# Attention's context kept with features on partitions up to the output projection; softmax denominators inverted by way of DMA hops and applied on GpSimd

## The reference, cut to what matters

```
x = x + layernorm(attention(layernorm(x)))
x = x + layernorm(experts(layernorm(x)))
```

```
scores = einsum('bhqd,bhkd->bhqk', q, k) / 4        # masked with -inf
ctx    = einsum('bhqk,bhkd->bhqd', softmax(scores), v)
out    = ctx.reshape(B, S, D) @ w_o.T + b_o
```

## Time and profile before

| What | us |
|---|---|
| median of 3 runs | 2270.2 (2268.99 to 2270.75) |
| the profiled execution's own time | 2272.05 |
| span of its trace, first to last instruction | 2270.3 |
| attention, first to last exponential and its end | 204 to 1241 |
| output projection and router | 1247 to 1420 |
| experts | 1420 to 2270 |

### The profile page before, as it was taken

How to read it: one execution, slowest core, us unless ns; L and a number is a source line. 1 busy time by engine, 2 the same in 40 slices (tenths; PEclk the granted TensorE clock), 3 DMA queues, 4 the chain that set the end, 5 groups by cost and what they waited for, 6 DMA issues and landing times. The chain is left out here.

```text
span 2270.3 us, 38461 instructions
## 1 busy us (share of the span) xinstructions
PE 2092.2 (92%) x14097; PEld 1282.3 (56%) x14097; DVE 1477.1 (65%) x2381; ACT 1697.8 (75%) x2165; POOL 654.8 (29%) x648
## 2 busy tenths in 40 slices
PE   7995999999999999999998797999999999999970
PEld 6773333333333333333333796888888888888860
DVE  5663255555555655455555796876788888888865
ACT  5664999999999999999998574333466666666645
POOL 1111000000000000000000343776146566555637
PEclk9997999999999999999999796999999999999985
DMA  6886745555444445555420684564477776667756
GB/s 216 308 295 187 125 61 76 77 74 76 63 61 56 61 67 76 76 74 76 54 42 9 230 274 158 186 244 159 174 220 188 179 198 172 169 173 180 181 171 246
DMA packets 161574, 324.37 MB, mean 143 GB/s; under 512 B 18000, under 2 KB 91856, under 8 KB 155632
## 3 DMA queue, kind: packets, MB, share of 16 engines
q1 hardware_dynamic: 128820, 268.13, 45.9%
q0 software_dynamic: 30256, 46.03, 10.9%
q10 hardware_dynamic: 2316, 7.80, 0.9%
HBM read 198.75 MB, written 127.47 MB: 144 GB/s over the span
## 5 line engine op out<-in xcount | busy, mean ns | idle before, releaser
L1112 ACT ACTIVATE att_prob<-att_scores 128x1024 f32<-128x1024 f32 (+2 forms) x1122 | 997.8, 1031 | 57.5 <-PE att_scores L1059 53.8
L1078 PE MATMUL att_out<-att_prob,att_va 128*32 128x512 f32 (+3 forms) x5000 | 576.8, 542 | 12.5 <-DVE att_prob L1144 12.2
L1059 PEld LDWEIGHTS att_scores<-att_qs,att_ks 50*128 50x128 f32 x2560 | 211.0, 185 | 494.6 <-ACT att_prob L1112 416.7
L1059 PE MATMUL att_scores<-att_qs,att_ks 50*128 50x512 f32 (+3 forms) x2560 | 465.6, 430 | 22.9 <-PEq L118 17.3
L1829 POOL DMA_INDIRECT sums<-moe_y,moe_token x142 | 303.1, 2135 | 256.7 <-ACT moe_y L2113 212.3
L1010 POOL DMA_DIRECT2D ctx_scr<-att_cout x64 | 55.1, 861 | 980.7 <-DVE att_cout L1194 941.7
L1144 DVE SCALAR_TENSOR_TENSOR att_prob<-att_prob,att_tri 128x512 f32<-128x512 f32 x224 | 144.7, 687 | 266.3 <-ACT att_prob L1112 266.3
L1078 PEld LDWEIGHTS att_out<-att_prob,att_va 128*32 128x32 f32 x5000 | 108.8, 108 | 185.5 <-issue 103.3
L1983 PE MATMUL moe_ps<-moe_xt_hi,w_first_hi 128*128 128x512 f32 (+1 forms) x448 | 175.9, 393 | 3.8 <-ACT moe_h L2086 2.1
L1983 PE MATMUL moe_ps<-moe_xt_hi,w_first_lo 128*128 128x512 f32 (+1 forms) x448 | 172.5, 385 | 0.0
L1983 PE MATMUL moe_ps<-moe_xt_lo,w_first_hi 128*128 128x512 f32 (+1 forms) x448 | 172.5, 385 | 0.0
(11 more groups left out here) (295 smaller groups left out, 3930.4 us busy)
## 6 DMA issues: line engine op xcount, KB each, us to landing
qk_parts<-proj_qk SPq DMA_DIRECT2D x64, 512.0 KB, 4.6
keep_first_weights<-w_experts SPq DMA_DIRECT2D x22, 1412.0 KB, 6.7
moe_wraw<-w_experts SPq DMA_DIRECT2D x21, 1412.0 KB, 6.7
att_qs<-qk_parts SPq DMA_DIRECT2D x180, 128.0 KB
att_ks<-qk_parts SPq DMA_DIRECT2D x180, 128.0 KB
moe_rows<-rows_in SPq DMA_DIRECT2D x22, 544.0 KB, 3.9
proj_xin<-x SPq DMA_DIRECT2D x16, 512.0 KB, 3.8
v_scr<-proj_va SPq DMA_DIRECT2D x16, 512.0 KB, 3.5
```

The lines of the kernel that those rows point to most:

```text
L1059: last = nc.tensor.matmul(pss[e % SBUFS][:, h, at:at + CH - q0], ks[s][rows, half, kt * P:(kt + 1) * P], qs[s][rows, half, c * CH + q0:(c ...
L1078: last = nc.tensor.matmul(pso[k % 2][strip, q0:], va[team % 2][:, kt, strip], probs_of(u)[:, h, at:at + CH - q0], start=(kt == 0), stop=(i ...
L1112: nc.scalar.activation(probs_of(u)[:, half * 2:half * 2 + 2, start:], pss[e % SBUFS][:, :, start:], ACT.Exp, scale=HD ** -0.5)\
```

## The change

In attention, `turn` and `finish` are gone. The values take the first 16 of 32 columns and all other columns are ones. `copy` writes `osb` with the 512 queries in another order and waits for the store of chunk k-2. From `osb` SP moves the 4 rows of denominators to a tile of 32 partitions by 64 (`move_denominators`, a DMA on q1), VectorE inverts it (`invert`, five units after the chunk's end), and GpSimd, for one chunk after the other: stores the inverses to DRAM, waits, loads them spread over 32 partitions for each head, waits, multiplies `osb` in place (128x512), and stores all 128 partitions (256 KB) to `ctx_rows`. The product of chunk k waits for `copy` of chunk k-2. The move of a team's first chunk stands in SP's list between the loads of the next team's queries and those of its keys; the moves of its second and third stand behind all of these loads, and the move of its fourth ahead of the next loads.

In the output projection the 8 transposes and `psT` are gone: two DMAs load 16 of each 32 rows of `ctx_rows`, features on partitions, and `context_hi` and `context_lo` read that tile.

```diff
+def load_features(eng, to, rows, done):
+
+    teams = TEAMS // KT
+    for k in range(KT):
+        each = rows[k * teams:(k + 1) * teams].rearrange("a (h r) t -> (a h) r t", r=VA_W)
+        eng.dma_start(to[:, k], each[:, 0:HD]).then_inc(done, 16)
+
+
+FEATURE_LOADS = KT
...
-    ctx_scr = dram("ctx_scr", (T, D))
+    ctx_rows = dram("ctx_rows", (NCH, TEAMS, P, CH))
...
+    inv_scr = dram("inv_scr", (2, TEAM, CH))
...
 
 VALUES = 2
 COPY = VALUES
-TURN = VALUES + 1
-FINISH = VALUES + 1
+INVERT = COPY + 3
...
-        rden = ph.sb2("rden", [P, TPC * TEAM])
-        cout = ph.sb2("cout", [P, TPC, TEAM * HD])
+        dens = ph.sb2("dens", [TEAM * DEN_ROWS, CH // DEN_ROWS])
+        shares = ph.sb2("shares", [TEAM * DEN_ROWS, CH // DEN_ROWS])
+        inverse = ph.sb2("inverse", [P, CH])
...
+                for k in range(ALL_TEAMS * BCH):
+                    n, s = divmod(k, 2)
+                    pool.wait_ge(inverted[s], n + 1)
+                    pool.dma_start(inv_scr[s].rearrange("h (r t) -> (h r) t", r=DEN_ROWS), shares[s][:]).then_inc(kept[s], 16)
+                    pool.wait_ge(kept[s], (n + 1) * 16)
+                    pool.dma_start(inverse[s][:], inv_scr[s].unsqueeze(1).broadcast_to([TEAM, VA_W, CH])).then_inc(spread[s], 16)
+                    pool.wait_ge(spread[s], (n + 1) * 16)
+                    nc.gpsimd.tensor_tensor(osb[s][:], osb[s][:], inverse[s][:], ALU.mult).then_inc(c_done, 1)
+                    team, c = divmod(k, BCH)
+                    pool.wait_ge(c_done, k + 1)
+                    pool.dma_start(ctx_rows[team // TEAMS * BCH + c, team % TEAMS], osb[s][:]).then_inc(stored[s], 16)
                 for s in range(2):
                     pool.wait_ge(stored[s], ALL_TEAMS * BCH // 2 * 16)
...
+                def move_denominators(k):
+                    n, s = divmod(k, 2)
+                    sp.wait_ge(o_copied, k + 1)
+                    if n:
+                        sp.wait_ge(inverted[s], n)
+                    sp.dma_start(dens[s][:], osb[s][HD::VA_W].rearrange("h (r t) -> h r t", r=DEN_ROWS))\
+                        .then_inc(moved[s], 16)
+
                 for team in range(1, ALL_TEAMS):
+                    k = (team - 1) * BCH
                     if team > 1:
+                        move_denominators(k - 1)
                         sp.wait_ge(used, (team - 1) * NU)
-                    load_heads(sp, team, slice(0, BCH), loaded[team % 2])
+                    load_parts(sp, team, slice(0, BCH), loaded[team % 2], 0)
+                    move_denominators(k)
+                    load_parts(sp, team, slice(0, BCH), loaded[team % 2], 1)
+                    load_values(sp, team, slice(0, BCH), loaded[team % 2])
                     load_guard(sp, team)
...
+                    for c in range(1, BCH - 1):
+                        move_denominators(k + c)
+                for k in range((ALL_TEAMS - 1) * BCH - 1, ALL_TEAMS * BCH):
+                    move_denominators(k)
...
-                        wait_from_one(pe, c_done, k - 1)
+                        wait_from_one(pe, o_copied, k - 1)
...
-                def turn(k):
-                    pe.wait_ge(o_copied, k + 1)
-                    for j in range(TPC):
-                        last = nc.tensor.transpose(pso[k % 2][:, j * P:(j + 1) * P],
-                                                   osb[k % 2][:, j * P:(j + 1) * P], ident[:])
-                    last.then_inc(o_turned, 1)
-
-                for r in range(len(RING_UNITS) + TURN):
+                for r in range(len(RING_UNITS) + VALUES):
...
-                    if r >= TURN and RING_UNITS[r - TURN] in end_of:
-                        turn(end_of[RING_UNITS[r - TURN]])
...
-                    V.tensor_copy(va[s][:, tiles].rearrange("p t (h w) -> p (t h) w", w=VA_W)[:, :, 1:1 + HD],
+                    V.tensor_copy(va[s][:, tiles].rearrange("p t (h w) -> p (t h) w", w=VA_W)[:, :, 0:HD],
...
-                    V.memset(va[s][:], 0.0).then_inc(cleared, 1)
-                    dve.wait_ge(cleared, 2 * s + 1)
-                    V.memset(va[s][:].rearrange("p t (h w) -> p (t h) w", w=VA_W)[:, :, 0:1], 1.0)\
-                        .then_inc(cleared, 1)
-                    dve.wait_ge(cleared, 2 * s + 2)
+                    V.memset(va[s][:], 1.0).then_inc(cleared, 1)
+                    dve.wait_ge(cleared, s + 1)
...
-                    wait_from_one(dve, o_turned, k - 1)
-                    V.tensor_copy(osb[k % 2][:], pso[k % 2][:]).then_inc(o_copied, 1)
+                    wait_from_one(dve, stored[k % 2], k // 2 * 16)
+                    V.tensor_copy(osb[k % 2][:].rearrange("p (j q) -> p j q", j=TPC),
+                                  pso[k % 2][:].rearrange("p (q j) -> p j q", j=TPC)).then_inc(o_copied, 1)
...
-                def finish(k):
-
-                    dve.wait_ge(o_turned, k + 1)
-                    o = pso[k % 2][:].rearrange("p (g w) -> p g w", w=VA_W)
-                    V.reciprocal(rden[k % 2][:], o[:, :, 0]).then_inc(inverted, 1)
-
-                    wait_from_one(dve, stored[k % 2], k // 2 * 16)
-                    dve.wait_ge(inverted, k + 1)
-                    V.tensor_tensor(cout[k % 2][:].rearrange("p j (h d) -> p (j h) d", h=TEAM), o[:, :, 1:1 + HD],
-                                    rden[k % 2][:].unsqueeze(2).broadcast_to([P, TPC * TEAM, HD]),
-                                    ALU.mult).then_inc(c_done, 1)
+                def invert(k):
+
+                    n, s = divmod(k, 2)
+                    dve.wait_ge(moved[s], (n + 1) * 16)
+                    if n:
+                        dve.wait_ge(kept[s], n * 16)
+                    V.reciprocal(shares[s][:], dens[s][:]).then_inc(inverted[s], 1)
...
+                for r in range(len(RING_UNITS) + INVERT):
+                    if r >= INVERT and RING_UNITS[r - INVERT] in end_of:
+                        invert(end_of[RING_UNITS[r - INVERT]])
...
-                        sp.wait_ge(c_turned, c - 1)
-                    sp.dma_start(cin[c % 2][:], ctx_ch[c]).then_inc(c_loaded[c % 2], 16)
+                        sp.wait_ge(c_lo, c - 1)
+                    load_features(sp, cin[c % 2], ctx_rows[c], c_loaded[c % 2])
...
-                def turn(c):
-                    if c == 0:
-                        pe.wait_ge(first_loaded, 2 * 16)
-                    else:
-                        pe.wait_ge(c_loaded[c % 2], (c + 1) // 2 * 16)
-                    if c:
-                        pe.wait_ge(c_lo, c)
-                    transposes(nc, psT, cin[c % 2], ident).then_inc(c_turned, 1)
...
-                    if chunk(k):
-                        turn(k)
...
-                    act.wait_ge(c_turned, c + 1)
+                    if c == 0:
+                        act.wait_ge(first_loaded, (FEATURE_LOADS + 1) * 16)
+                    else:
+                        act.wait_ge(c_loaded[c % 2], (c + 1) // 2 * FEATURE_LOADS * 16)
                     if c >= 2:
                         act.wait_ge(o_done, 2 * (c - 1))
-                    nc.scalar.activation(ct[c % 2][0][:], psT[:], ACT.Copy).then_inc(c_hi, 1)
...
-                    V.tensor_tensor(ct[c % 2][1][:], psT[:], ct[c % 2][0][:].bitcast(F32), ALU.subtract)\
+                    V.tensor_tensor(ct[c % 2][1][:], cin[c % 2][:], ct[c % 2][0][:].bitcast(F32), ALU.subtract)\
```

More of the change, by code:

```diff
@@ L37 @@
 VA_W = 32
+DEN_ROWS = 8
 STRIP_W = 32
@@ L249, in load_out_first @@
                     sp.dma_start(out_bias[:], bcast(b_o, 0, [P, D])).then_inc(out_loaded, 16)
-                    sp.dma_start(out_cin[:], ctx_run[0]).then_inc(out_loaded, 16)
-                attend(nc, ident, norms, qk_parts, v_scr, guard, qk_stored, v_stored, ctx_ch, blank, rows_in, sums, load_out_first)
+                    load_features(sp, out_cin, ctx_rows[0], out_loaded)
+                attend(nc, ident, norms, qk_parts, v_scr, guard, qk_stored, v_stored, ctx_rows, inv_scr, blank, rows_in, sums, load_out_first)
                 late = whole.enter_context(nc.sbuf_tensor("late", [P, LATE], F32, side="right"))
@@ L836, with attend @@
 POLY = 10
-def attend(nc, ident, norms, qk_parts, v_scr, guard, qk_stored, v_stored, ctx_ch, blank, rows_in, sums, load_out_first):
+def attend(nc, ident, norms, qk_parts, v_scr, guard, qk_stored, v_stored, ctx_rows, inv_scr, blank, rows_in, sums, load_out_first):
     with ExitStack() as ctx:
@@ L924, in attend @@
         SR = (T + CH - FIRST * CH) // P // 2
[L925 to L927 removed]
+        assert TPC <= SR <= ZR
+        zeros = ph.sb("zeros", [P, SR, RW])
+        spare = ph.sb("spare", [P, SR], I32)
         z_made, z_stored = ph.sem("zeros_made"), ph.sem("zero_rows_stored")
@@ L934, in attend @@
         late_read, late_step, late_done = ph.sem("late_scores_read"), ph.sem2("late_steps"), ph.sem("late_probs_ready")
-        o_copied, o_turned = ph.sem("out_copied"), ph.sem("out_turned")
-        inverted, c_done = ph.sem("denominators_inverted"), ph.sem("context_done")
```

(19 more changed lines are left out.)

19 lines of the change are left out of this document (7 added, 12 removed).

## The result

Median of 4 runs 2585.74 us (2580.39 to 2587.28), against 2270.22 for the kernel before: ratio 1.139, 95% interval 1.1377 to 1.1405, slower by 315.5 us. The profiled execution has a span of 2583.3 us, 313.0 more than before. The forecast said slower by 197, within 2390 to 2550: the direction was right, the size fell outside the range.

The account below looks back on a forecast made before the run. ScalarE was taken to bound attention and VectorE the projection. Terms -4.4 (turn gaps), +177.8 (14 teams), +18.7 (team 0), +7.3 (attention's end), -2 (projection) sum to +197.4: 2468 us, range 2390 to 2550.

Parts of the forecast that it names:

- The bound and the mechanism: Attention: ScalarE bounds; second chunk's copy waits for an earlier store, inversion for SP's move; shift 10.1 us per team.
- ScalarE loses 2 us: First chunk of a team: the move lands behind query loads, TensorE's values come 2.2 us late, ScalarE loses 2 us.
- my bound of 4: First chunk of a team: upper bound on ScalarE's loss, 4 us; lower bound 0.
- the moves without a long chain: Second chunk of a team: with a short GpSimd chain, its move behind all loads alone shifts the team 8.0 us.
- Spread and store are 256 KB: 9.1 each: GpSimd chain beside the loads: spread and store each take 9.1 us, as a 128 KB store there does.
- my upper bound of 13.6: GpSimd chain beside the loads: longest hop taken as 13.6 us, giving a shift of 14.5 us per team.
- The clock: TensorE behind the second chunk's stall: two units at low clock, 2.6 us per team; bounds 0 and 4.7.
- Team 0: First team: moves queue behind loads, masks come 12.3 and 6.4 us late, +18.7 us; bounds 8 and 25.
- End of attention: Behind the last copy: move, reciprocal, write, spread and multiply uncovered, +7.3 us; bounds 5 and 12.
- both branches of my own term: Output projection: first 8 transposes go, -2 us; up to +5 if the clock fell for want of TensorE work.
- Rival A: Attention: GpSimd's hops short beside the loads, only the moves hold VectorE; 2402 us, 2438 with clock term; chance 0.25.

Follow-up runs that it names:

- run 9: Changed kernel with the moves ahead of the loads' halves and neither write nor spread (GpSimd multiplies by ones): 2278.6 us, ratio 1.0035.
- run 14: Changed kernel, two context tiles, first two chunks' moves sent first, next team's loads held until the first chunk's spread landed: 2291.6 us, ratio 1.0098.
- Run 6: Changed kernel without the write to DRAM and the spread, GpSimd multiplying by ones; moves, inversions, multiplies and stores stay: 2454.3 us.
- Run 4: Changed kernel with the spread reading 128 separate rows of 2 KB instead of four rows 32 times each: 2520.1 us.
- run 8: Changed kernel with the moves ahead of the loads' halves and without GpSimd's multiply: 2439.2 us.
- run 1: Changed kernel with three context tiles instead of two: 2488.5 us.
- run 5: Changed kernel with three context tiles and the moves ahead of the loads' halves: 2431.6 us.
- run 10: Changed kernel, three context tiles, loads held until the first chunk's spread, second move between query and key loads, inversions and value placement later: 2447.3 us.
- run 13: Changed kernel, three context tiles, first two chunks' moves sent first, next team's loads held until the first chunk's spread landed: 2289.9 us, ratio 1.0090.
- run 11: Changed kernel with the projection's 8 transposes per chunk back, read by the low part from PSUM: 119.2 us from first to last low part.
- run 12: Changed kernel with the projection's 8 transposes per chunk back, read by nobody: 119.3 us from first to last low part.
- run 2: Changed kernel with each inversion five ring steps later in VectorE's list: 2607.3 us.

## Why the prediction was wrong in size

- **The bound and the mechanism: right, for attention.** ScalarE was the bound, the copy of the second chunk waits for the store of the chunk two before it and the inversion for the move. With the moves put forward and the hops gone (run 9), or with the loads held back (run 14), nothing of it is left in a team.
- **"ScalarE loses 2 us" at the first chunk: the step that failed first.** From the loads' start (forecast at 598.2, measured at 547.58) the inversion came after 16.1 us, forecast 14.1, and the mask was due 0.8 us earlier: the first chunk's copy came 4.1 us behind the loads' start, where I had 4.9. Together TensorE's values came some 5 us late, not 2.2 (it idled 5.36 us), and in that idle time its granted clock fell to 0.50, a fall I had put at the second stall only: the first values behind it took 1.94 us for 1.07. ScalarE lost 6.67 us, beyond my bound of 4. Run 6 has the moves' cost alone, the first's and the second's: 10 us a team. The forecast's bound for that case, the moves without a long chain, was 8.0.
- **"Spread and store are 256 KB: 9.1 each": the largest miss.** The write took 8.7 us at the median (forecast 7; 9.0 in the team shown), the store only about 2.3, when the burst was over, and the spread 20.6, far beyond my upper bound of 13.6. The copy came 38.0 us behind the loads' start, forecast 30.4. I had priced the spread by a store of half its bytes. Run 4 shows that its pattern is the lesser part (5.7 us).
- **The clock: right in kind, short in length.** In the team shown TensorE worked at half speed for 9.4 us behind the second hole and for 4.7 behind the first; the upper bound was 11 in all. No run separates what that costs from the holes themselves.
- **Team 0: the cause right, the size by luck**, 19.3 for 18.7. There the moves alone act: without the hops (run 6) its last copy comes at the same time, 295.26 for 295.30. But the mask behind the first move came 17.0 us late (240.47 for 223.48) where I had 12.3, and the mask behind the second only 3.0 more (263.26 for 243.27) where I had 6.4.
- **End of attention: 17.9 for 7.3.** From the last copy to the store's issue 15.4 us (forecast 9.8; before 2.5): the 8 KB write takes 5.2 to the spread's issue and the spread 5.3 to the multiply, on a quiet bus where I had 2.4 and 2.8. Then 9.0 us to the next stage for 3.8: after its last wait GpSimd's drain instruction lasts 5.53 us, before 0.38. I had no term for that. Its cause is open: it stays without the multiply (5.53, run 8) and without the hops (5.28, run 6), but in all four kernels with three context tiles (runs 1, 5, 10 and 13) it lasts 1.04 us, and from the last store's issue to the next stage it is 4.4 us instead of 9.0.
- **Projection: both branches of my own term came.** I took -2 and named up to +5 if the clock fell for want of TensorE's work. The first 8 transposes gave their 2 us (the first low part comes 1.2 us into the stage, before 3.2), and the clock fell: +5.5 from the first to the last low part, which runs 11 and 12 take back. The table's +1.9 is these two and 1.7 us that come back behind. VectorE alone did not bound the stage, as I had read: its busy time hardly changed (101.9 for 101.0 us) and the stage grew.
- **Rival A** (hops short beside the loads) is refuted by the 20.6 us. The Trainium skill, DMA: Bandwidth & Descriptors, section "Queues, rings and completion order", has a DMA engine take turns between queues packet by packet. The trace agrees in part: of the spread issued at 560.47, the first packet moved at 571.62, 11.1 us later, while SP's queue moved about 140 packets in every 2 us as before; from then on both queues' packets ran mixed until 580.3. The turns came only after a wait that the rule does not have; on a quiet bus a spread's first packet moved 1.3 us behind its issue. What that wait was for no run shows; VectorE was busy for 2.9 of the 11.1 us.

## What to carry to other kernels

What a small DMA costs the engine that waits for it depended here on what stood in the queues at its issue far more than on its bytes (8 KB: 2.0 us to landing on a quiet bus, 8.7 in the burst). Before adding one, mark on the timeline when the bulk loads are issued and drain, and put the small one's issue and its wait outside that stretch. Here the same moves and hops cost 274 us over 14 teams inside it, and nothing that a team's time shows when the bulk loads were sent some 20 us later in a team of 64 us. A wait that is taken away can come back as another one on the same engine: later inversions took 184 us off one wait of VectorE and the copy's grew by 79, and the kernel was 22 us slower (run 2). Prices come from removing each cost alone and both together. Work removed from TensorE can lower its clock, so it is not free to remove: here 5.5 us of a stage of 120.

## What the runs showed of the hardware that I had not expected

- A DMA on GpSimd's queue, issued while SP's queue is full, moved nothing for 11.1 us (spread, 256 KB) and about 5 us (write, 8 KB); on a quiet bus it was 1.3 and 0.6 us.
- Reading four rows of 2 KB 32 times each takes 5.3 us from issue to landing on a quiet bus, with at most 6 packets of 4 KB under way at a time; reading 128 separate rows takes 3.0, with up to 19; storing 128 rows 2.3.
- GpSimd's 128x512 multiply takes 1.26 us alone and 12.3 beside VectorE's polynomial steps (run 6; at most 13.0, run 13). Of GpSimd's 32 `out_rstd` (128x4) 14 go from 1.04 to 1.86 us when VectorE's low part reads both operands from SBUF (runs 11 and 12).
- GpSimd's drain at the end of attention: 0.38 us before, 5.53 in the changed kernel, 1.04 with three context tiles.
